# Decoder layer on one core: the first attention batch in another order, with queries six steps in front

## The reference

```python
xn = _layernorm(x, g_norm)                     # x is already normalised once
q = xn @ Wq                                    # 512 -> 16 heads x 128
k, v = split(xn @ Wkv)                         # one key head, one value head of 128
q, k = _l2norm(q * SCALE), _l2norm(k)          # each row by its own norm
sim = einsum('bhid,bjd->bhij', q * s, k * s)   # s = sqrt(16)
out = einsum('bhij,bjd->bhid', softmax(sim), v)
x = x + _layernorm(out @ Wout, g_out)
# then: each token through the expert of its id (4 experts), ctx as gate, up and down weights
# then: two linear layers whose weights are rounded to -1, 0, 1 by scale 1 / mean(|w|)
```

## Time and profile before

| what | before |
|---|---|
| time, median of 3 | 1055.99 us |
| profiled execution: time | 1056.72 us |
| its span | 1054.9 us |
| PE busy | 929.9 us (88%) |
| DVE busy | 696.9 us (66%) |
| ACT busy | 632.7 us (60%) |
| POOL busy | 229.9 us (22%) |
| granted PE clock, mean | 0.965 |

### The profile page before, as it was taken

One profiled execution on the slowest core, in us unless ns is written; L12 is line 12 of the kernel. 1 busy time (PEld: TensorE's weight loads), 2 busy tenths in 40 slices (PEclk: granted clock), 3 DMA queues, 4 the chain that ended last, 5 costly groups with the idle time before them and its releaser, 6 DMA issues.

```text
span 1054.9 us, 18958 instructions
## 1 busy us (share of the span) xinstructions
PE 929.9 (88%) x6522; PEld 519.1 (49%) x6538; DVE 696.9 (66%) x1540; ACT 632.7 (60%) x1601; POOL 229.9 (22%) x401
## 2 busy tenths in 40 slices
PE   0678879879999998999999999999874969999983
PEld 0335545546565665565656565666431324444431
DVE  4248986676887575877748676778252457777762
ACT  2547676766676574667666767665112159887751
POOL 1202111111232132232221212121141012323331
PEclk9989999999999999999999999999996989999998
DMA  8414556464676444547534444359926986544432
GB/s 270 90 39 112 139 116 126 82 140 131 160 166 165 121 116 106 106 119 150 112 81 116 111 106 102 105 126 166 239 101 144 186 140 158 108 90 91 107 81 77
DMA packets 305663, 131.85 MB, mean 125 GB/s; under 512 B 275233, under 2 KB 279841, under 8 KB 305569
## 3 DMA queue, kind: packets, MB, share of 16 engines
q1 hardware_dynamic: 301728, 118.03, 51.2%
q0 software_dynamic: 3840, 12.60, 3.4%
HBM read 42.76 MB, written 20.99 MB: 60 GB/s over the span
## 4 chain that ended last, share of the span: by engine, by line
PE 65%; DVE 10%; ACT 7%; SPq 5%; issue 5%; DMA 5%; POOL 2%; ACTq 0%; POOLq 0%
PE QB L238 6%; PE QB L240 6%; PE QB L239 6%; PE S L656 5%; PE OUTB L668 5%; PE S L240 4%; PE S L239 4%; PE S L238 4%; PE O L565 4%; PE O L563 4%; PE O L567 4%; PE OUTB L238 4%; PE OUTB L239 4%; PE OUTB L240 4%; DVE P L1081 2%
## 5 line engine op out<-in xcount | busy, mean ns | idle before, releaser
L565 PE MATMUL O<-V,P 128*128 128x128 f16 x1024 | 179.2, 221 | 0.0
L563 PE MATMUL O<-V,P 128*128 128x129 f16 x1024 | 179.0, 219 | 0.0
L567 PE MATMUL O<-V,P 128*128 128x129 f16 x1024 | 178.9, 218 | 0.0
L1081 DVE TENSOR_TENSOR P<-P 128x1024 f16<-128x1024 f32 x128 | 156.8, 1225 | 4.4
L774 ACT ACTIVATE OTOK<-O,rd 128x128 f16<-128x128 f32 x256 | 79.5, 365 | 133.3 <-DVE rd L1086 133.2
L1069 DVE SCALAR_TENSOR_TENSOR QTOKR<-QB,rn,QTOKR 128x128 f16<-128x128 f32 x240 | 67.6, 344 | 118.8 <-ACT QTOKR L755 118.7
L763 ACT ACTIVATE P<-S,cst 128x1024 f32<-128x1024 f32 x128 | 139.9, 1131 | 10.0 <-PE S L240 9.7
L238 PE MATMUL QB<-WQA,XQA 128*128 128x512 f16 x240 | 95.0, 396 | 36.7 <-DVE QTOKR L1069 23.0
L1387 POOL TENSOR_SCALAR qst<-qs 128x4 f32<-128x4 f32 x64 | 18.6, 291 | 495.5 <-ACT junk L746 488.6
L565 PEld LDWEIGHTS O<-V,P 128*128 128x128 bf16 x1024 | 99.2, 97 | 7.4
L563 PEld LDWEIGHTS O<-V,P 128*128 128x128 bf16 x1024 | 98.4, 96 | 7.8 <-issue 0.4
(11 more groups left out here) (191 smaller groups left out, 1866.5 us busy)
## 6 DMA issues: line engine op xcount, KB each, us to landing
SIDE<-in_L_ffn_w_dram SPq DMA_DIRECT2D x64, 256.0 KB, 3.2
OTA<-sorted_rows SPq DMA_DIRECT2D x4, 1028.0 KB, 8.0
OTA<-in_L_attn_Wq_dram SPq DMA_DIRECT2D x4, 1024.0 KB, 11.6
SIDE<-in_L_attn_Wout_dram SPq DMA_DIRECT2D x16, 256.0 KB, 2.9
SIDE<-in_ctx_dram SPq DMA_DIRECT2D x16, 256.0 KB, 3.2
ctx_split<-SIDE SPq DMA_DIRECT2D x16, 256.0 KB, 2.9
ROWB<-in_x_dram SPq DMA_DIRECT2D x16, 256.0 KB, 3.1
w_tern<-SIDE SPq DMA_DIRECT2D x32, 128.0 KB, 2.7
```

The lines of the kernel that those rows point to most:

```text
L563: nc.tensor.matmul(o, ph(g)[:, a:a + P], V[:, b % 2, j, 0:129], start=j == 0, stop=False)
L565: nc.tensor.matmul(o[:, 0:128], ph(g)[:, a:a + P], V[:, b % 2, j, 130:258], start=False, stop=False)
L567: last = nc.tensor.matmul(o, pl(g)[:, a:a + P], V[:, b % 2, j, 0:129], start=False, stop=j == NT - 1)
L1081: nc.vector.tensor_tensor(pl(g)[:, cols], P32[:, cols], ph(g)[:, cols], ALU.subtract).then_inc(p_lo, 1)
```

## The change

Queries are made six steps in front instead of five, and their tiles alternate between the banks QB and OUTB up to tile 19. In a step ScalarE now does the squares of the next query tile before the exponentials and its scaling behind them, instead of scaling before and squares behind; VectorE does the query remainder between the two halves of the probabilities instead of in front of both. The start is written in another order on all engines: statistics and normalisations of x skewed against each other, the transposes of x in front of most Wq loads, Wq's second quarter rounded by VectorE alone, its last in single pieces over steps 1 to 5, routing in front of step 0, keys and values of the first batch read straight from PSUM. The g_out load is issued by GpSimd. Keys of later batches go to the first score bank. All |w| sums stand in steps 14 to 29, two a step. The all-reduce becomes a matmul with float32 ones in step 32.

```diff
-AHEAD = 5
+AHEAD = 6
...
         def qbank(u):
-            return S[:, u * 512:(u + 1) * 512] if u < 4 else QB[:, :]
+            return S[:, u * 512:(u + 1) * 512] if u < 4 else OUTB[:, :] if u % 2 and u < 20 else QB[:, :]
         def kvbank(n):
-            return O[:, n * 512:(n + 1) * 512] if n < 2 else QB[:, :]
+            return O[:, n * 512:(n + 1) * 512] if n < 2 else S[:, 0:512]
         def kvf(n):
-            return XSR[:, n % 2, :]
+            return kvbank(n) if n < 2 else XSR[:, n % 2, :]
         def piece_at(g):
-            return [p for p in range(2 * HEADS) if p - (p >= HEADS) == g]
+            return [p for p in range(2 * HEADS) if HEADS - 2 + p // 2 == g]
...
 # SP
-            sp.dma_start(GO[:, :], g_out.partition_broadcast(P)).then_inc(go_in, 16)
-            for h in range(2):
-                load_wout(h)
-                load_sum(h)
+            load_wq(0)
             for k in range(NT):
                 turn_x(k)
+            for q in range(1, 3):
+                load_wq(q)
             turn_k(0)
             for u in range(NT):
                 turn_q(u)
+            load_wq(3)
+            for h in range(2):
+                load_wout(h)
+            turn_q(4)
...
-                if g + 4 < STEPS:
-                    turn_q(g + 4)
...
+                if g + 5 < STEPS:
+                    turn_q(g + 5)
                 if g >= 1:
                     turn_o(g - 1)
+                for p in piece_at(g + 1):
+                    load_sum(p)
...
 # PE, queries(u)
-                if u >= 5:
-                    pe.wait_ge(q_lo, u)
-                for n in range(2, 8):
-                    if kv_at(u - AHEAD) == n:
-                        pe.wait_ge(kv_f, n + 1)
+                if 6 <= u < 20:
+                    pe.wait_ge(q_lo, u - 1)
+                elif u >= 20:
+                    pe.wait_ge(q_lo, u if u > 20 else 19)
...
 # PE, scores(g)
+                    if half == 0 and kv_at(g - 1) is not None:
+                        pe.wait_ge(kv_f, kv_at(g - 1) - 1)
...
 # PE, outputs(n)
-                    pe.wait_ge(wo_lo, HEADS)
-                    pe.wait_ge(pos_ready, 2)
+                    pe.wait_ge(q_lo, 20)
+                if t == 0 and b == 0:
+                    pe.wait_ge(wo_lo, 4 * (q + 1))
...
 # PE, the steps
                 scores(g)
+                if g == 0:
+                    pe.wait_ge(pos_ready, 1)
+                    queries(5)
+                if g == 2 * HEADS:
+                    pe.wait_ge(w_scale, 1)
+                    pe.wait_ge(out_cp, 4)
+                    nc.tensor.matmul(OUTB[:, 0:2], onesf[:, :], wsc[:, 0:2], start=True, stop=True
+                                     ).then_inc(w_total, 1)
                 if g >= 1:
                     values(g - 1)
                 if kv_at(g) is not None:
                     keys_values(kv_at(g))
+                if g >= HEADS:
+                    outputs(g - HEADS)
                 if g + AHEAD < STEPS:
                     queries(g + AHEAD)
-                if g >= HEADS:
-                    outputs(g - HEADS)
...
 # ACT, the steps
-                if g + 4 < STEPS:
-                    query_high(g + 4)
+                if g >= 1 and g + 5 < STEPS:
+                    query_squares(g + 5)
                 for half in range(2):
                     exponentials(g, half)
+                if g == 0:
+                    query_squares(5)
+                if g + 5 < STEPS:
+                    query_high(g + 5)
+                if g >= 1:
+                    head_high(g - 1)
                 if kv_at(g) is not None:
                     kv_copy(kv_at(g))
-                if g >= 1:
-                    head_high(g - 1)
-                if g + AHEAD < STEPS:
-                    query_squares(g + AHEAD)
...
-                if g in (0, 3):
-                    query_weights(2 + g // 3)
+                if 1 <= g < 1 + DC:
+                    query_weight(3, g - 1)
...
 # DVE, the steps
-                if g + 4 < STEPS:
-                    query_low(g + 4)
                 probabilities(g, 0)
+                if g == 2 * HEADS:
+                    weight_scales_set()
                 if g >= 1:
                     head_sums(g - 1, 0)
+                if g + 5 < STEPS:
+                    query_low(g + 5)
                 probabilities(g, 1)
...
 # POOL
+            nc.gpsimd.dma_start(GO[:, :], g_out.partition_broadcast(P)).then_inc(go_in, 16)
...
-                if g == 2 * HEADS - 1:
-                    pool.wait_ge(w_scale, 1)
-                    nc.gpsimd.partition_all_reduce(wsc[:, 2:4], wsc[:, 0:2], P, RADD).then_inc(w_total, 1)
```

More of the change, by code:

```diff
@@ L16 @@
 AX = mybir.AxisListType
-RADD = bass.bass_isa.ReduceOp.add
 P = 128
@@ L372, in _, with load_wq @@
             sp.dma_start(wkv_st, Wkv.rearrange("(c p) n -> p c n", p=P)).then_inc(wkv_in, 16)
-            for q in range(4):
+            def load_wq(q):
                 sp.dma_start(OTA[:, q * 2048:(q + 1) * 2048].rearrange("p (c n) -> p c n", c=DC),
@@ L598, in _ @@
             keys_values(1)
-            for u in range(AHEAD):
+            pe.wait_ge(counts, 2)
+            nc.tensor.matmul(OUTB[:, 0:E * TILES], lower[:, :], scm[:, :], start=True, stop=True)
+            nc.tensor.matmul(OUTB[:, 64:64 + E * TILES], onesb[:, :], scm[:, :], start=True, stop=True
+                             ).then_inc(rank_ps, 1)
+            for u in range(5):
                 queries(u)
@@ L840, in _ @@
                     last.then_inc(wkv_hi, 1)
-            query_weights(0)
-            for n in range(2):
-                kv_copy(n)
-                key_squares(n)
-            for n in range(2):
-                key_high(n)
-                value_high(n)
+            for c in range(DC):
+                query_weight(0, c)
+            key_squares(0)
+            key_squares(1)
+            key_high(0)
+            value_high(0)
+            key_high(1)
+            value_high(1)
             query_squares(0)
@@ L852, in _ @@
             query_squares(2)
+            query_high(2)
             query_squares(3)
-            query_high(2)
             query_high(3)
-            query_weights(1)
             query_squares(4)
+            for c in range(DC):
+                query_weight(2, c)
+            query_high(4)
             for g in range(STEPS):
@@ L1179, in _ @@
             last.then_inc(wkv_lo, 1)
-            query_weights(0)
+            input_norm(3)
+            input_low(2)
+            input_low(3)
+            for c in range(DC):
+                query_weight(0, c)
+            routing_counts()
+            routing_places()
             for n in range(2):
                 key_low(n)
-            for n in range(2):
                 value_low(n)
-            for u in range(NT):
-                query_low(u)
-            query_weights(1)
+            for c in range(DC):
+                query_weight_high(1, c)
+            for c in range(DC):
+                query_weight(1, c)
+            query_low(0)
+            query_low(1)
+            routing_pairs()
+            query_low(2)
+            query_low(3)
+            for c in range(DC):
+                query_weight(2, c)
+            query_low(4)
             for g in range(STEPS):
@@ L1414, in _ @@
                 input_rstd(k)
+            nc.gpsimd.dma_start(GO[:, :], g_out.partition_broadcast(P)).then_inc(go_in, 16)
             for n in range(2):
                 key_norm(n)
-            for u in range(AHEAD):
+            for u in range(5):
                 query_norm(u)
             for g in range(STEPS):
+                if g + 5 < STEPS:
+                    query_norm(g + 5)
+                if kv_at(g - 1) is not None:
+                    key_norm(kv_at(g - 1))
+                if prep_at(g, 2) is not None:
+                    input_rstd(prep_at(g, 2))
+                if out_at(g, 1) is not None:
+                    out_rstd(out_at(g, 1), 0, o_mv, OUT_EPS, o_rs)
+                if out_at(g, 2) is not None:
+                    out_rstd(out_at(g, 2), 1, h_mv, EPS, h_rs)
                 if out_at(g, 2) is not None:
```

96 lines of the change are left out of this document (42 added, 54 removed).

## The result

| what | before | after |
|---|---|---|
| time, median (lowest to highest) of 4 | 1055.78 us (1053.61 to 1056.77) | 1021.72 us (1016.09 to 1028.94) |
| ratio, 95% interval | | 0.968 [0.9652, 0.9708] |
| profiled execution: time, span | 1056.72, 1054.9 | 1022.30, 1020.6 |

The forecast was 1019, range 1004 to 1036. In the tables Ex is the start of the first exponential of step x, from ScalarE's timelines.

What follows compares the result with a forecast made beforehand. It took the start as bound by SP's queue, first-batch steps by a ScalarE and VectorE ring, later batches as near TensorE's bound. Savings 18.5 + 9.7 + 9 = 37.2 us off 1056.7 gave 1019.5, median forecast 1019, range 1004 to 1036.

Steps and rivals of the forecast that it cites:

- Start: Stretch up to the third exponential: earlier transposes of x and keys bring it from 83.85 to 65.4 us, 18.5 saved.
- Steps 2 to 15: First batch: fourteen rings of 8.37 plus extras sum to 133.6 us against 143.3, 9.7 saved.
- 8.37 + 1.77 + 0.63: Early first-batch steps: quiet step 8.37, plus 1.77 for x rounding's wait and work, plus 0.63 for a Wq piece.
- E16: Sign at the end of the first batch: step 16's first exponential starts near 199 us, against 227.16 before.
- The wait of queries is gone since two banks alternate, but it is not what holds the ring.: Steps 2 to 15: alternating banks end the queries' wait, but the ring through ScalarE and VectorE sets the step.
- Rival (a): Steps 2 to 15: queries' bank was the true bound, so 17.4 us more saved, 1002; chance 0.08.
- TensorE's 116.2: Steps 2 to 15: TensorE's bound, 14 x 7.93 + 5.2 of keys, would save 27 us.
- the ring of 8.37: Quiet first-batch step: the new order's closed chain of ScalarE and VectorE work, 8.37 us a step.
- The norm (1.55): GpSimd's norm after the squares: kept at 1.55 us, lying under two exponentials of 2.05.
- the rival: Shared port rule: norm longer by 1.85, leaving cover by 1.35 in 14 steps, 1043 us; chance 0.04.
- Batches 1 to 3: Later batches: 3.2 + 3.1 + 4.8 = 11.1 us removable, 2 lost in batch 1, 9 saved.
- 1.56 each: Two key stretches of the later batches: keys go to a score bank, saving 1.56 us in each.

Runs made afterwards that it cites:

- e5: Changed kernel with SP's loads at the start in the old order, all Wq loads and g_out before the transposes of x; ratio 0.9766.
- e1_again: The changed kernel measured once more with no edit; 1019.98 us, ratio 0.9659.
- e8: Changed kernel with later rounding of x and h, start squares moved before the preceding tile's scaling, routing's pairs in step 0; 1013.9 us, ratio 0.9598.
- e9: Changed kernel with both the old ScalarE and VectorE step order and one bank for queries from tile 4 on; 1035.78 us, ratio 0.9789.
- e3: Changed kernel with the sums of |w| one a step from step 0 on, as before; 1027.49 us, ratio 0.9719.
- e6: Changed kernel with all queries from tile 4 on in the one bank QB, still six steps in front; 1033.44 us, ratio 0.976.
- e2: Changed kernel with the old step order on ScalarE and VectorE from step 1 on; banks, sums and start stay new; 1032.01 us, ratio 0.9764.
- e4: Changed kernel with ScalarE's rounding of x and h one step later, between squares and exponentials; 1017.31 us, ratio 0.963.
- e10: Changed kernel with the keys of batches 1 to 3 in the queries' bank QB again; 1035.75 us, ratio 0.9782.

## Why the prediction was right, point by point

- **Start (18.5; 17.9).** The cause was in the main the queue of SP: the first key product is 13.7 us earlier, and e5 gives 10 of them back by three Wq loads and g_out. From this product to E0 it takes 32.3 us (31.4 in e1_again) where it took 34.7; which part of the new order on the other engines gives these 2 to 3 us was not tried. The first key product came at 14.5, not 15.5: the prediction read the 8.04 of the earlier trace rows as the arrival of g_norm, but VectorE did not wait there, and g_norm was in at 7.00. Keys ended 0.5 late, E0 came 1.0 late and in e1_again 0.2 early. The sum had the norms of query tiles 2 and 3 (1.5 each; ScalarE stands 1.41 and 1.40); no term names the first wait, 1.23 for tile 1, and the squares of tile 2 end at 33.6, not 32.5. e8 takes these waits away.
- **Steps 2 to 15 (9.7; 9.6).** By e9 some 6.4 us of this come from what left the steps and 3.8 from order and bank together. Quiet steps 8.35 (8.37), steps 2 and 4 at 10.74 and 10.88 (8.37 + 1.77 + 0.63 = 10.8), steps 6 and 8 at 10.64 and 10.13 (8.37 + 1.77 = 10.1), E16 at 199.66 (199). e3 shows that a sum costs 0.6 there, the lower end that was given (0.61 to 0.75).
- **A step that failed: "The wait of queries is gone since two banks alternate, but it is not what holds the ring."** It holds for the old order, where the second bank is worth 0.1 us in steps 2 to 15, and not for the new, where it is worth 5.3; with steps 0 and 1 e6 loses 10.7 us. Rival (a) was rightly held low as it stood, since two banks did not bring TensorE's 116.2; but the ring of 8.37 stands on the second bank. The forecast was not hurt because the change had both.
- **The norm (1.55).** It takes 1.7 us from the end of the squares and is covered by 0.08. Its line has a median of 1385 ns, where the earlier trace rows show 1034; with the old order (second row, e2) it is 1012:

```profile
L1428 POOL TENSOR_TENSOR rn<-qst,half x64: 1006/1385/1970, 27.1 to 653.5; 128x4 f32<-128x4 f32 x64
```
```profile
L1431 POOL TENSOR_TENSOR rn<-qst,half x64: 1006/1012/1989, 26.1 to 660.6; 128x4 f32<-128x4 f32 x64
```

  So the new place does lengthen it. In steps 2 to 15 it takes 1.33 to 1.41 us in 13 of 14 steps of the changed kernel, 1.01 in 12 of 14 of e2. These longer ones begin 0.4 to 0.7 us before a cast of VectorE and all end behind it, mostly by 0.04 us (the quiet step above: cast to 144.16, norm to 144.21), and the norms of e4 beside which no cast runs take 1.01 again (its median is 1.04). The longest, 1.97 and in e2 1.99, stand in the first two steps with either order and begin under a subtraction that has 1.1 us to go. It is never the 1.85 more of a half that the rival charged, and it costs the steps nothing. The Trainium skill ("SBUF — State Buffer", "Who interferes with whom") names a shared port pair that the loser waits for; the traces agree as far as one cast or subtraction goes, but no run here shows a block as long as both.
- **Batches 1 to 3 (9; 10.0 up to E63).** Batch by batch the sum has 2.8, 6.4 and nothing; measured are 1.7 (2.8 in e1_again), 6.4 and 1.9. The close total is in part luck, since its terms are off both ways. The all-reduce was worth 5.3 in step 32 (4.8). Steps 16 to 19, for whose stretch 3.2 was put down, are 0.3 shorter (1.4 in e1_again). Steps 27 and 28 are 4.7 shorter and 43 and 44 3.3, where 1.56 each was charged, and by e10 the bank is 3.6 and 2.1 of it; but steps 20 to 26 are 2.9 longer than before and 33 to 42 1.6, with TensorE full (it lacks 1.2 us in all from 200 to 700), so work is only moved between neighbours and the net gain of the key stretches is smaller. The 1.9 of batch 3 had no term: steps 58 to 62 take 40.9 for 43.0. With queries six in front, step 57 is the last to make any, before it was step 58, and the product (2.58 at most) has moved to the start, where TensorE stands. No experiment took the sixth step back, so this last point is a reading of the program and the steps, not shown by a run.
- **What was given back (0; -3.2).** The prediction followed the time to the end of attention and took the rest as fixed. E63 is 37.5 us earlier, but the last transpose of head outputs only 35.6. SP's queue around step 63, before and after:

```profile
742.08 1.26 SPq L317 DMA_TRANSPOSE OTA<-OTOK  x1
...
744.01 4.11 SPq L421 DMA_TRANSPOSE WQA<-ctx_split  x1
...
750.08 1.25 SPq L317 DMA_TRANSPOSE OTA<-OTOK  x1
```
```profile
705.04 1.27 SPq L319 DMA_TRANSPOSE OTA<-OTOK  x1
...
706.99 5.58 SPq L427 DMA_TRANSPOSE WQA<-ctx_split  x1
...
714.53 1.25 SPq L319 DMA_TRANSPOSE OTA<-OTOK  x1
```

  In both SP stands nowhere between these rows: its queue is full, with 8.0 us from the transposes of one head to those of the next before and 9.5 after. The last of them is issued 18.5 us behind E63 before, 20.4 after. In this profile the transpose of ctx in front of it takes 5.58 instead of 4.11, but that is not the cause of all: in e1_again it takes 4.12, and the last transpose still is 19.9 behind E63. So 1.4 to 1.9 of the 3.2 us are lost in this queue, the rest behind it. Since the part behind E63 varies by 6.5 us between the executions of the new kernels and there is one profile of before, how much of the 3.2 belongs to the change is open; no experiment moved it.

## What to carry to other kernels

A ring of engines has more than one closing path: an order of work and a second buffer may each be worth nothing alone (here -1.6 and 0.1 us over 14 repeated steps) and something together (3.8), so they are tried together, and in both single forms, and the first steps are counted apart. Work that was free under a wait (the |w| sums) has a price once the wait is reordered away, so it has to move in the same change. A prediction should follow the time to the last instruction: here 3.2 us of 37.5 were not there at the end, 1.4 to 1.9 of them in a queue in program order that was full behind the improved part.

## What the runs showed of the hardware

- The all-reduce on GpSimd has a record of 0.73 us, and the engine then stood 7.59 us; the cost is behind the record.
- The GpSimd power of 128 x 4 elements takes 1.01 us by itself, and 1.33 to 1.41 in the changed kernel (1.10 and more in e3) where VectorE's cast of 1024 columns starts 0.4 to 0.7 us behind it: mostly it then ends 0.04 us behind the cast, which takes its 0.69 all the same. In e4, where some of these casts came later, the same norms took 1.01.
- The g_out load, 128 x 512, took SP 8.49 us to issue where it stood behind the Wq loads (before and e5).
- The fp32 product with two columns has a record of 0.28 us (bounded before by 2.58 and zero), and step 32 is no longer than its neighbours by more than 0.13 (10.65 against 10.52).
